# The output projection of a transformer layer, moved from a phase of its own into the attention loop

## The chip, the cores and the metric

The kernel runs on one core of a Trainium2 chip. The metric is the time of one execution on the device in microseconds. TensorE is called PE, VectorE DVE, ScalarE ACT, GpSimd POOL, and SyncE, which issues nearly all DMAs, SP.

## The reference

A layer on x (16 batches, 1024 tokens, width 256, float32): a modulated layer norm, attention with a residual, and a mixture of eight experts on the first two batches' tokens. Cut to what the change touches:

```
# q, k, v: [16 batches, 16 heads, 1024, 16], rotary embedding applied to q and k
scores = einsum('bhid,bhjd->bhij', q, k) / sqrt(16)
scores = scores * mask + (1 - mask) * -1e9            # causal
probs  = softmax(scores, axis=-1)
out    = einsum('bhij,bhjd->bhid', probs, v)          # then heads side by side: [16, 1024, 256]
out    = out @ Wo + bo
x      = x + ga * (h + out)                           # ga: a gate, one row of 256 per batch
```

## The kernel before, in words

`build` (L61) runs five phases, one after the other. Phase 0 prepares weights and the modulation rows, phase 1 makes q, k and v and stores them and the residual in DRAM, phase 2 (L717) is the attention, phase 3 (L1106) the output projection, phase 4 the experts. Each phase is a block in which the five engines run their own instruction lists, written out by hand in `@block.sync`, `@block.gpsimd` and so on, and meet by semaphores only. An engine works strictly in its list's order, so a wait holds up all that is queued behind it on that engine. At a phase's end all engines and outstanding DMAs meet.

Phase 2 works through 64 units: unit u = 4b + g is batch b and group g of four heads. Within a unit PE does two things in turn. For its own unit it computes transposed scores in ten pieces of up to 512 queries, four heads each (`scores_for_exp`, L1045). ACT takes the exponential of each (L992, from one of three PSUM banks), POOL zeroes the masked part of the six pieces on the diagonal, pieces 0, 1, 2, 7, 8 and 9 (`select`, L879), and two pieces later PE multiplies by the values (`weigh`, L1056). `weigh` of piece 7 therefore stands at the end of piece 9, the last of the unit, and those of pieces 8 and 9 in the next unit. The values carry columns of ones, so a head gives 16 rows of numerators and rows of the sum of its exponentials, the denominator. Between its score matmuls PE computes, for the unit two ahead, the plain scores whose row maxima DVE takes (`fill`, L1008, in 40 fillings, two for each of 20 slots; `largest`, L931). Slot 4 (`TURN`) holds no scores: its first filling transposes the maxima of the unit before (`turn_max`, L1039), its second is empty. The maxima are negated and split into three bf16 parts by DVE (L921) and POOL (`parts`, L888), and SP stores them to DRAM and loads them back as three more rows of q (`maxima`, L838), which is needed at the start of the next unit.

SP's list in a unit (`step`, L856) is: wait until the unit before has been weighed, load q, k and v for the unit four after it (nine DMAs for q and k, one for v, 2 MB), store the second half of the unit before, `maxima` of the next unit, store the first half of this unit (numerators and denominators unnormalised, in `att_d`, 512 KB a unit).

Phase 3 loads a batch of `att_d` (2 MB, double buffered) and the residual (1 MB), and goes through eight tiles of 128 tokens: PE transposes the tile's four groups (L1215), DVE takes the reciprocals of the denominators (L1180) and multiplies (L1184), PE transposes the product (two, L1223), ACT copies it (L1201), PE multiplies by the gated Wo, after a bf16 matmul for the bias (L1233, L1235), DVE adds the residual (L1190), and SP stores the batch.

Of the kernel before, what the change touches and what calls it, by code (L numbers as in the profile page):

```python
# [25 lines left out]
P = 128  # L26
# [34 lines left out]
def build(nc, a, out):  # L61
# [21 lines left out]
    max_d = nc.dram_tensor("neg_max", [NG, 3, HG * T, P], BF16, kind="Internal").ap()  # L83
    att_d = nc.dram_tensor("att", [B, NG, P, L], F32, kind="Internal").ap()
# [3 lines left out]
    with ExitStack() as outer:  # L88
# [12 lines left out]
        phase2(nc, B, L, ps, ident, mask, q_d, k_d, v_d, max_d, att_d)  # L101
        phase3(nc, B, L, D, ps, ident, wo, ones3, mods_d, out_bias_d, resid_d, att_d, sum_d, out)
# [614 lines left out]
def phase2(nc, B, L, ps, ident, mask, q_d, k_d, v_d, max_d, att_d):  # L717
    T = L // P
    DH = q_d.shape[3] // HG
# [44 lines left out]
    PS_A, PS_B, PS_O = 0, 4, 7  # L764
    BANKS = 3
# [3 lines left out]
    with ExitStack() as ctx:  # L769
# [13 lines left out]
        o_sb = sb("o_sb", [P, 2, HALF], F32)  # L783

# [9 lines left out]
        o_stored = many("p2_o_stored", 2)  # L794
        block = ctx.enter_context(nc.Block())

        LAST = B - 1

# [26 lines left out]
        def _(sp):  # L825
# [24 lines left out]

            def prologue():
                for n in range(UNITS):
                    load(unit(0, n))
                maxima(unit(0, 0))

            def step(un, ahead):  # L856
                b, g, u = un
                final = isinstance(b, int) and b == LAST
                if not (isinstance(b, int) and b == 0 and g == 0):
                    was = prior(un)  # L860
                    if not (final and g):

                        wait_apart(sp, pv_done, was[2] * NPC + NPC)
                        load(unit(was[0], was[1] + NG))
                    store(was, 1)
                if not (final and g == NG - 1):
                    maxima(unit(b, g + 1))
                store(un, 0)

            def epilogue():  # L870
                store(unit(LAST, NG - 1), 1)
                for c in range(2):
                    sp.wait_ge(o_stored[c], B * NG * DMA)
# [4 lines left out]
        def _(pool):  # L878
# [17 lines left out]

            def step(un, ahead):
                for i in range(NPC):
                    if diag(PIECES[i]):
                        select(un, i)  # L900
                    if i == 3 and ahead is not None:
                        parts(prior(ahead))
                if ahead is None and un[1] == NG - AHEAD:
# [7 lines left out]
            steps(pool, prologue, step)  # L911

        @block.vector
        def _(dve):
# [46 lines left out]
            def step(un, ahead):  # L961
                if ahead is not None:
                    whole(ahead)
                elif un[1] == NG - AHEAD:
# [6 lines left out]
            steps(dve, prologue, step)  # L971
# [35 lines left out]
        def _(pe):  # L1007
            def fill(un, n, first=False):  # L1008
# [30 lines left out]
            def turn_max(un):  # L1039
# [3 lines left out]
                             ident[:, :]).then_inc(turned, 1)  # L1043

# [38 lines left out]
            def step(un, ahead, first=False):  # L1083
                for i in range(NPC):
                    for h in range(HG):
# [17 lines left out]

def phase3(nc, B, L, D, ps, ident, wo, ones3, mods_d, out_bias_d, resid_d, att_d, sum_d, out):  # L1106
    T = L // P
    KC = D // P
    DH = D // HEADS
    SB = (sum_d.shape[0] - P) // L  # L1110
    PS_A, PS_T, PS_C = 0, 2, 4
    with ExitStack() as ctx:
        sb = lambda n, s, d: ctx.enter_context(nc.sbuf_tensor(n, s, d))
        sem = lambda n: ctx.enter_context(nc.semaphore(n))
        pair = lambda n: (sem(n + "0"), sem(n + "1"))
        att = sb("att_b", [P, 2, NG, L], F32)
        res = sb("res_b", [P, 2, T, D], F32)
        gate = sb("gate_b", [P, 2, D], F32)
        ob = sb("ob_b", [3, 2, D], BF16)
        wg = sb("wg", [P, 2, KC, D], F32)  # L1120
        rec = sb("rec", [P, 2, HEADS], F32)
        norm = sb("norm", [P, 2, D], F32)
        n_t = sb("n_t", [P, 2, KC, P], F32)
        x2 = sb("x2", [P, 2, T, D], F32)
        att_in, small_in, res_in = pair("p3_att_in"), pair("p3_small_in"), pair("p3_res_in")
        wg_done = sem("p3_wg")
        at_done, rec_done, norm_done = sem("p3_at"), sem("p3_rec"), sem("p3_norm")
        nt_done, nt_copied = sem("p3_nt"), sem("p3_nt_copied")
        c_done, x2_done = sem("p3_c"), sem("p3_x2")
        stored = pair("p3_stored")  # L1130
        block = ctx.enter_context(nc.Block())

        def loop(eng, work):
            for p in range(2):
                work(p, 0, p)
            for it in range(1, B // 2):
                for p in range(2):
                    work(it * 2 + p, it, p)

        def load(sp, b, p):  # L1140
            sp.dma_start(att[:, p], att_d[b].rearrange("g p t -> p g t")).then_inc(att_in[p], DMA)
            sp.dma_start(res[:, p], resid_d[b]).then_inc(res_in[p], DMA)
# [466 lines left out]
```

## Time and profile before

| | |
|---|---|
| time of 3 executions | 3256.54, 3257.68, 3258.6 us |
| the profiled execution | 3256.85 us, its span 3255.1 us |
| PE, DVE, ACT, POOL busy | 91%, 72%, 53%, 31% of the span |
| phase 2: first load of v to ACT's last copy | 767 to 2627 us |
| phase 3, to the first load of phase 4 | 2627 to 2915 us |

The profile is one execution. Busy shares are means over phases with different limits, so a stage is read by a table of stretches, and the order of things within a unit by the timeline. A number in square brackets after an instruction is the time that its engine stood idle before it, and what released it. The granted clock of PE is a share of 2.4 GHz; 0.50 is 1.2 GHz.

### The profile page before, as it was taken

Reading aid. Unit: us, or ns where it says so; the run is one execution under the profiler, and the core shown is the slowest. Engines: PE = TensorE matmul, PEld = TensorE weight load, DVE = VectorE, ACT = ScalarE, POOL = GpSimd, SP = SyncE. Lnnn points to the kernel's source line nnn. Section 1 sums busy time; section 2 is a strip of 40 time slices with the busy share of each in tenths; the row PEclk is TensorE's granted clock in tenths of the full one; section 3 lists DMA queues with packets and bytes.
Section 4 is the critical chain, followed back from the end, with each engine's and each line's share of the span. In section 5 each row is a group of like instructions: output and inputs, shape, how many; then the busy total and the mean of one; then the engine's idle time right before and its main releaser. Section 6 shows DMA issues by size and latency. Waiting matters only on the chain. (4 is left out here: it accounts for less than half of the span.)

```text
span 3255.1 us, 50330 instructions
## 1 busy us (share of the span) xinstructions
PE 2952.9 (91%) x18199; PEld 1403.3 (43%) x18199; DVE 2328.9 (72%) x3444; ACT 1713.4 (53%) x3591; POOL 1019.2 (31%) x1366
## 2 busy tenths in 40 slices
PE   2888998885999999999999999999999979975997
PEld 0444444441444444444444444444444347753664
DVE  5999999995777777777777777777777425543221
ACT  1444444430677777777777777777777731111111
POOL 3888888862122111112221111112221100003232
PEclk7999999996999999999999999999999989987999
DMA  2466666657244444444444444444444246663332
GB/s 77 138 180 191 191 191 191 184 156 175 55 95 93 95 100 100 100 96 92 94 95 92 97 100 100 100 96 90 95 92 92 48 173 259 259 230 110 78 100 56
DMA packets 175373, 403.11 MB, mean 124 GB/s; under 512 B 34556, under 2 KB 87202, under 8 KB 158518
## 3 DMA queue, kind: packets, MB, share of 16 engines
q1 hardware_dynamic: 168984, 391.37, 47.1%
q0 software_dynamic: 6144, 8.52, 1.5%
q8 instruction: 147, 2.41, 0.3%
q14 instruction: 98, 0.80, 0.1%
HBM read 240.65 MB, written 161.31 MB: 123 GB/s over the span
## 5 line engine op out<-in xcount | busy, mean ns | idle before, releaser
L946 DVE TENSOR_REDUCE mx<-ps 128x2 f32<-128x1024 f32 (+3 forms) x1216 | 1371.2, 1166 | 396.6 <-PE ps L1034 301.3
L992 ACT ACTIVATE prob<-ps 128x512 f32<-128x512 f32 (+1 forms) x2560 | 1251.4, 561 | 539.0 <-PE ps L1052 530.0
L1027 PE MATMUL ps<-k_rows,q_rows 96*128 96x512 bf16 (+3 forms) x3072 | 909.9, 332 | 40.6 <-DMA k_rows<-k_parts 33.1
L1052 PE MATMUL ps<-q_rows,k_rows 99*128 99x512 bf16 (+3 forms) x3072 | 908.5, 329 | 14.5 <-ACT prob L992 6.0
L885 POOL TENSOR_SCALAR_AFFINE_SELECT prob<-prob 128x512 f32<-128x512 f32 x512 | 318.6, 634 | 1453.8 <-ACT prob L992 1453.8
L1071 PE MATMUL ps<-prob,v_rows 128*32 128x512 f32 (+3 forms) x6144 | 628.6, 497 | 0.0
L1052 PEld LDWEIGHTS ps<-q_rows,k_rows 99*128 99x128 bf16 x3072 | 273.3, 98 | 598.8 <-ACT prob L992 359.8
L688 PE MATMUL ps<-w_all,x_t 128*128 128x512 f32 (+1 forms) x1024 | 427.9, 543 | 0.0
L1027 PEld LDWEIGHTS ps<-k_rows,q_rows 96*128 96x128 bf16 x3072 | 290.4, 98 | 269.8 <-DVE mx L946 60.4
L1034 PE MATMUL ps<-mask_b,unit_b 128*128 128x128 bf16 (+2 forms) x1408 | 348.5, 248 | 0.0
L1071 PEld LDWEIGHTS ps<-prob,v_rows 128*32 128x32 f32 x6144 | 134.7, 108 | 245.7 <-ACT prob L992 122.8
L688 PEld LDWEIGHTS ps<-w_all,x_t 128*128 128x128 f32 x1024 | 183.5, 200 | 125.4 <-issue 104.0
L481 DVE TENSOR_TENSOR qr<-m 128x256 f32<-128x256 f32 x256 | 224.2, 958 | 4.4
L641 POOL TENSOR_TENSOR stage<-rest,stage 128x512 bf16<-128x512 f32 x128 | 167.5, 1308 | 119.3 <-ACT stage L575 119.2
L1201 ACT COPY n_t<-ps 128x256 f32<-128x256 f32 x128 | 47.6, 372 | 232.7 <-PE ps L1223 232.7
L1469 DVE SCALAR_TENSOR_TENSOR y<-ps,gx,gate 128x256 f32<-128x256 f32 x32 | 15.5, 484 | 195.7 <-PE ps L1560 192.3
L1034 PEld LDWEIGHTS ps<-mask_b,unit_b 128*128 128x128 bf16 x1408 | 139.2, 99 | 22.8
L1235 PE MATMUL ps<-wg,n_t 128*128 128x256 f32 x512 | 145.7, 407 | 0.0
L561 ACT COPY v_st<-ps 128x256 f32<-128x256 f32 x128 | 47.7, 373 | 178.1 <-PE ps L688 178.1
L675 PE MATMUL ps<-ident,xn 128*128 128x128 f32 x256 | 55.9, 304 | 87.1 <-DVE xn L461 87.1
L1190 DVE TENSOR_TENSOR x<-ps,res_b 128x256 f32<-128x256 f32 x128 | 54.3, 425 | 106.2 <-PE ps L1235 106.2
L1560 PE MATMUL ps<-w,hid 128*128 128x256 f32 x512 | 119.1, 386 | 0.0
(143 smaller groups left out, 2707.4 us busy)
## 6 DMA issues: line engine op xcount, KB each, us to landing
k_rows<-k_parts SPq DMA_DIRECT2D x384, 128.0 KB, 7.5
v_ones<-v_st SPq DMA_DIRECT2D x64, 512.0 KB, 9.0
v_rows<-v_ones SPq DMA_DIRECT2D x64, 512.0 KB, 9.5
att<-o_sb SPq DMA_DIRECT2D x128, 256.0 KB, 3.2
att_b<-att SPq DMA_DIRECT2D x16, 2048.0 KB, 10.9
q_parts<-stage SPq DMA_DIRECT2D x192, 128.0 KB, 2.4
k_parts<-stage SPq DMA_DIRECT2D x192, 128.0 KB, 2.4
q_rows<-q_parts SPq DMA_DIRECT2D x64, 384.0 KB, 4.6
```

The source lines that it names most:

```text
L481: ins = dve.tensor_tensor(dst[:, :, :, :, e], src(m1)[:, :, :, :, e], src(m2)[:, :, :, :, 1 - e], ALU.add)
L641: pool.tensor_tensor(stage[:, p, 2, :, t * P:(t + 1) * P], rest[:, t % 2, :].rearrange("p (a n) -> p a n", a=4), stage[:, p, 1, :, t * P:( ...
L688: ins = pe.matmul(o, x_t[:, t % 2, k, :], w_all[:, k, lo:hi], start=False, stop=(k == KC - 1))
L885: pool.affine_select(out=own, in_=own, compare_op=ALU.is_ge, fill=0.0, base=0, pattern=[[0, HG], [1, P]], channel_multiplier=-1).then_inc( ...
L946: dve.tensor_reduce(dst, src, AX.X, ALU.max).then_inc(a_free, 1)
L992: nc.scalar.activation(prob[:, (g * NPC + i) % RING, h, 0:w], src, ACT.Exp).then_inc(exp_done, 1)
L1027: ins = pe.matmul(ps[:, at, col:col + w], q[0:ROWS, g, h, i * P:(i + 1) * P], k[0:ROWS, g, h, k0:k0 + w], start=(r == 0), stop=True, skip_ ...
L1034: ins = pe.matmul(own, unit_b[:, :], mask_b[:, :].rearrange("p (o n) -> p o n", o=1) .to_broadcast([P, per, P]), start=False, stop=True, s ...
L1052: ins = pe.matmul(ps[:, PS_B + bank(g, n), at:at + w], k[0:AUG, g, h, j * P:(j + 1) * P], q[0:AUG, g, h, q0:q0 + w], start=True, stop=True)
L1071: ins = pe.matmul(ps[32 * h:32 * h + 32, PS_O, col:col + w], v[:, g, j, h, :], prob[:, (g * NPC + i) % RING, h, at:at + w], start=(j == 0) ...
L1235: ins = pe.matmul(o, n_t[:, r % 2, k, :], wg[:, p, k, :], start=False, stop=(k == KC - 1))
L1560: ins = pe.matmul(o, hid[:, f, c * P:(c + 1) * P], w2[:, e % 2, f, :], start=False, stop=(f == FT - 1))
```

## The change

Phase 3 is gone; its work is done inside phase 2. The numerators and denominators are not loaded as tokens by heads and transposed, but fetched out of `att_d` in the layout that the projection's stationary operand wants: 8 heads x 16 numerator rows make the 128 partitions of `num`, twice. The denominators of a batch come as one tile of 128 x 128 (`den`), DVE inverts it (`invert`), SP stores it to DRAM and loads it back with each head's row spread over that head's 16 partitions (`rec_b`), and POOL multiplies (`normalise`). The matmul then takes `num` as it is. The unit of the projection is a job j: two tiles of 128 tokens, four jobs to a batch, into one PSUM bank.

Where it all stands: SP fetches batch b - 1 in unit (b, 0), after `maxima`; saves and spreads the reciprocals in unit (b, 1), before and after `maxima`; stores the finished rows of batch b - 2 in unit (b, 2), after its last store. DVE inverts at slot 5 and makes the gated Wo at slot 12 of unit (b, 1), and adds a job's rows at slot 4. POOL normalises batch b - 1 in unit (b, 1) between `parts` and the selection of piece 7. PE does job u - 6 in unit u, in the empty second filling of slot 4, and slot 6, which uses that bank next, waits for the addition. The last six jobs and all that batch 15 needs follow the loop.

The diff, without declarations and without the removed phase 3:

```diff
         LAST = B - 1
+        BEHIND = 6
+        PAIRS = T // 2
+        JOBS = B * PAIRS
+        assert PAIRS == NG and TURN % 2 == 0
+        def job_of(u):
+            return u - BEHIND if u >= BEHIND else None
...
+            def fetch(b):
+                p, half = b % 2, b // 2
+                for c in range(2):
+                    sp.wait_ge(o_stored[c], (b + 1) * NG * DMA)
+                rows = att_d[b].rearrange("g (h n) t -> (g h) n t", h=HG)
+                reuse(sp, rec_done, b)
+                sp.dma_start(den[:, :], rows[:, DH, :].rearrange("h (x t) -> h x t", t=P)).then_inc(den_in, DMA)
+                reuse(sp, out_done, (b - 1) * PAIRS)
+                for k in range(KC):
+                    sp.dma_start(num[:, p, k, :], rows[8 * k:8 * k + 8, 0:DH, :]).then_inc(num_in[p], DMA)
+                sp.dma_start(gate[:, p], mods_d[b, M_GA, :].partition_broadcast(P)).then_inc(small_in[p], DMA)
+                sp.dma_start(ob[:, p], out_bias_d[b]).then_inc(small_in[p], DMA)
+                reuse(sp, x2_stored[p], half * DMA)
+                sp.dma_start(res[:, p], resid_d[b]).then_inc(res_in[p], DMA)
+            def save_reciprocals(b):
+                sp.wait_ge(rec_done, b + 1)
+                sp.dma_start(rec_d[b % 2].rearrange("h (x t) -> (h x) t", t=P), rec[:, :]).then_inc(rec_saved, DMA)
+            def spread_reciprocals(b):
+                sp.wait_ge(rec_saved, b * DMA + DMA)
+                reuse(sp, att_ready, b * PAIRS)
+                for k in range(KC):
+                    src = rec_d[b % 2, 8 * k:8 * k + 8, :].rearrange("h (o t) -> h o t", o=1).to_broadcast([8, DH, L])
+                    sp.dma_start(rec_b[:, k, :], src).then_inc(rec_in, DMA)
+            def store_rows(b):
+                sp.wait_ge(x2_done, (b + 1) * PAIRS)
+                dst = sum_d[b * L:(b + 1) * L] if b < SB else out[b]
+                sp.dma_start(dst.rearrange("(t p) d -> p t d", p=P), res[:, b % 2]).then_inc(x2_stored[b % 2], DMA)
...
+                if g == 1 and b >= 1:
+                    save_reciprocals(b - 1)
                 if not (final and g == NG - 1):
                     maxima(unit(b, g + 1))
+                if g == 0 and b >= 1:
+                    fetch(b - 1)
+                if g == 1 and b >= 1:
+                    spread_reciprocals(b - 1)
                 store(un, 0)
+                if g == 2 and b >= 2:
+                    store_rows(b - 2)
             def epilogue():
                 store(unit(LAST, NG - 1), 1)
-                for c in range(2):
-                    sp.wait_ge(o_stored[c], B * NG * DMA)
+                fetch(LAST)
+                save_reciprocals(LAST)
+                spread_reciprocals(LAST)
+                store_rows(LAST - 1)
+                store_rows(LAST)
+                for p in range(2):
+                    sp.wait_ge(x2_stored[p], DMA * (B // 2))
...
+            def normalise(b):
+                pool.wait_ge(num_in[b % 2], (b // 2 + 1) * KC * DMA)
+                pool.wait_ge(rec_in, (b + 1) * KC * DMA)
+                for r in range(PAIRS):
+                    at = slice(r * 2 * P, (r + 1) * 2 * P)
+                    pool.tensor_tensor(num[:, b % 2, :, at], num[:, b % 2, :, at], rec_b[:, :, at], ALU.mult) \
+                        .then_inc(att_ready, 1)
             def step(un, ahead):
                 for i in range(NPC):
                     if diag(PIECES[i]):
                         select(un, i)
                     if i == 3 and ahead is not None:
                         parts(prior(ahead))
+                    if i == 6 and un[1] == 1 and un[0] >= 1:
+                        normalise(un[0] - 1)
                 if ahead is None and un[1] == NG - AHEAD:
                     parts(unit(LAST, NG - 1))
...
-            def whole(un, first=False):
+            def invert(b):
+                dve.wait_ge(den_in, b * DMA + DMA)
+                reuse(dve, rec_saved, b * DMA)
+                dve.reciprocal(rec[:, :], den[:, :]).then_inc(rec_done, 1)
+            def gated(b):
+                dve.wait_ge(small_in[b % 2], (b // 2 + 1) * (2 * DMA))
+                reuse(dve, out_done, (b - 1) * PAIRS)
+                for k in range(KC):
+                    ins = dve.tensor_tensor(wg[:, b % 2, k, :], wo[:, k, :], gate[:, b % 2, :], ALU.mult)
+                ins.then_inc(wg_done, 1)
+            def add_rows(j, bank):
+                b, r = j // PAIRS, j % PAIRS
+                rows = res[:, b % 2, 2 * r:2 * r + 2, :]
+                dve.wait_ge(res_in[b % 2], (b // 2 + 1) * DMA)
+                dve.wait_ge(out_done, j + 1)
+                dve.tensor_tensor(rows, ps[:, bank, :].rearrange("p (r n) -> p r n", r=2), rows, ALU.add) \
+                   .then_inc(x2_done, 1)
+            def whole(un, now=None, first=False):
                 for s in range(NS):
-                    if s == 2 and not first:
+                    if now is not None and now[1] == 1 and now[0] >= 1 and s == 5:
+                        invert(now[0] - 1)
+                    if now is not None and now[1] == 1 and now[0] >= 1 and s == 12:
+                        gated(now[0] - 1)
+                    if un is not None and s == 2 and not first:
                         finish(prior(un))
-                    if s != TURN:
+                    if un is not None and s != TURN:
                         largest(un, s)
-                    elif not first:
+                    elif un is not None and not first:
                         negate(prior(un))
+                    if s == TURN and now is not None and job_of(now[2]) is not None:
+                        add_rows(job_of(now[2]), PS_OUT)
...
+                whole(ahead, now=un)
+            def epilogue():
+                for j in range(JOBS - BEHIND, JOBS):
+                    if j == LAST * PAIRS:
+                        invert(LAST)
+                        gated(LAST)
+                    add_rows(j, PS_TAIL[j % 2])
...
+                j = job_of(u - AHEAD)
                 if s == TURN:
                     if not first and half == 0:
                         pe.wait_ge(a_free, u * NR + s - 1)
                         turn_max(prior(un))
+                    if half == 1 and j is not None:
+                        project(j, PS_OUT)
                     return
                 if half == 0 and s - 2 == TURN:
                     reuse(pe, m_left, u)
+                    if j is not None:
+                        pe.wait_ge(x2_done, j + 1)
                 elif half == 0:
                     reuse(pe, a_free, u * NR + (real(s - 2) + 1 if s >= 2 else s - 1))
...
+            def project(j, bank):
+                b, r = j // PAIRS, j % PAIRS
+                if r == 0:
+                    pe.wait_ge(wg_done, b + 1)
+                    pe.wait_ge(small_in[b % 2], (b // 2 + 1) * (2 * DMA))
+                pe.wait_ge(att_ready, j + 1)
+                for t in (2 * r, 2 * r + 1):
+                    o = ps[:, bank, (t % 2) * D:(t % 2) * D + D]
+                    pe.matmul(o, ones3[:, :], ob[:, b % 2, :], start=(t % 2 == 0), stop=False, skip_group_check=True)
+                    for k in range(KC):
+                        ins = pe.matmul(o, num[:, b % 2, k, t * P:(t + 1) * P], wg[:, b % 2, k, :], start=False,
+                                        stop=(k == KC - 1), skip_group_check=True)
+                ins.then_inc(out_done, 1)
...
+                        if ahead is None and n == 9:
+                            pe.wait_ge(x2_done, job_of(un[2]))
+                            project(job_of(un[2]), PS_OUT)
...
                 weigh(unit(LAST, NG - 1), i)
+            for j in range(JOBS - BEHIND, JOBS):
+                pe.wait_ge(x2_done, j - 1)
+                project(j, PS_TAIL[j % 2])
```

## Rows read from the trace of the kernel before

**Rows 1.** The page: busy tenths of PE and its granted clock in 40 slices.
```profile
PE   2888998885999999999999999999999979975997
PEclk7999999996999999999999999999999989987999
```

**Rows 2.** By stretches: us, busy PE, PEld, DVE, ACT, POOL, clock, DMA, GB/s.
```profile
2431.09:2459.29 28.20, 28.14 (x220) 11.60 (x216) 21.99 (x23) 20.53 (x42) 5.62 (x10) 1.00 0.48 96
2629.00:2914.60 285.60, 253.66 (x1408) 191.52 (x1408) 149.53 (x416) 47.62 (x128) 0.00 (x0) 0.96 0.65 243
```

**Rows 3.** Timeline of PE in the projection phase: start us, us, engine, line.
```profile
2650.95 0.28 PE L1233 MATMUL ps<-ob_b,ones 3*128 3x256 bf16 x1
...
2652.12 0.60 PE L1215 MATMUL ps<-ident,att_b 128*128 128x128 f32 x4
...
2652.88 0.28 PE L1233 MATMUL ps<-ob_b,ones 3*128 3x256 bf16 x1
```

**Rows 4.** Timeline at the projection phase's two ends.
```profile
2626.41 0.58 ACT L980 COPY o_sb<-ps 128x512 f32<-128x512 f32 x1 [1.87 <-PE ps L1071]
...
2909.93 0.39 SPq L1150 DMA_DIRECT2D out<-x  x1
2914.63 0.37 SPq L1312 DMA_DIRECT2D x_all<-sum_rows  x1
```

**Rows 5.** Chain that ended last, just after the projection phase: start us, us.
```profile
2914.63 8.33 DMA x_all<-sum_rows
```

**Rows 6.** The same chain in the last phase.
```profile
2985.13 0.21 PE ps L1558
2985.34 3.65 PE ps L1560 x16
```

**Rows 7.** Timeline of PE within one unit, and at its end.
```profile
2437.84 0.22 PE L1034 MATMUL ps<-mask_b,unit_b 128*128 128x128 bf16 x1
2438.13 0.28 PE L1052 MATMUL ps<-q_rows,k_rows 99*128 99x256 bf16 x1
...
2458.29 1.06 PE L1071 MATMUL ps<-prob,v_rows 128*32 128x512 f32 x8
```

**Rows 8.** Groups of instructions by line: busy us, mean ns of one, idle before.
```profile
L641 POOL TENSOR_TENSOR stage<-rest,stage 128x512 bf16<-128x512 f32 x128 | 167.5, 1308 | 119.3 <-ACT stage L575 119.2
...
L474 DVE TENSOR_TENSOR m<-ps,rope 128x512 f32<-128x512 f32 x128 | 86.8, 678 | 7.6 <-PE ps L688 7.6
...
L234 DVE RECIPROCAL e<-e 16x256 f32<-16x256 f32 x1 | 1.7, 1741 | 0.0
```

**Rows 9.** Timeline of SP and POOL within the same unit.
```profile
2437.24 1.23 SPq L835 DMA_DIRECT2D q_rows<-q_parts  x3
...
2442.24 0.43 SPq L841 DMA_DIRECT2D neg_max<-m  x1
2451.83 0.25 SPq L843 DMA_DIRECT2D q_rows<-neg_max  x1
...
2453.32 0.63 POOL L885 TENSOR_SCALAR_AFFINE_SELECT prob<-prob 128x512 f32<-128x512 f32 x1 [12.92 <-ACT prob L992]
```

**Rows 10.** DMA issues by tile: size, median us to landing.
```profile
v_rows<-v_ones SPq DMA_DIRECT2D x64, 512.0 KB, 9.5
...
res_b<-resid SPq DMA_DIRECT2D x16, 1024.0 KB, 12.8
```

**Rows 11.** The tile xin, one load of 1024 KB: its landings.
```profile
DMA to landing us min/median/max: 5.4/7.7/8.9
```

**Rows 12.** Timeline at the one long pause of PE in the attention phase.
```profile
2600.12 1.91 PE L1052 MATMUL ps<-q_rows,k_rows 99*128 99x512 bf16 x4 [4.62 <-DMA q_rows<-neg_max]
```

**Rows 13.** Table by stretches about that pause (columns as in rows 2).
```profile
2596.00:2597.00 1.00, 0.00 (x0) 0.00 (x0) 0.00 (x0) 0.00 (x0) 0.42 (x1) 1.00 0.00 0
2597.00:2598.00 1.00, 0.00 (x0) 0.00 (x0) 0.00 (x0) 0.00 (x0) 0.00 (x0) 0.84 0.11 25
...
2604.00:2605.00 1.00, 0.96 (x6) 0.41 (x4) 0.00 (x0) 0.53 (x2) 0.00 (x0) 0.75 0.00 0
```

More of the change, by code:

```diff
@@ L83, in build @@
     max_d = nc.dram_tensor("neg_max", [NG, 3, HG * T, P], BF16, kind="Internal").ap()
+    rec_d = nc.dram_tensor("rec_den", [2, HEADS, L], F32, kind="Internal").ap()
     att_d = nc.dram_tensor("att", [B, NG, P, L], F32, kind="Internal").ap()
@@ L100, in build @@
         phase1(nc, x, ps, ident, rope, w_all, bias3, ones3, mods_d, resid_d, q_d, k_d, v_d)
-        phase2(nc, B, L, ps, ident, mask, q_d, k_d, v_d, max_d, att_d)
-        phase3(nc, B, L, D, ps, ident, wo, ones3, mods_d, out_bias_d, resid_d, att_d, sum_d, out)
+        phase2(nc, B, L, D, ps, ident, mask, wo, ones3, mods_d, out_bias_d, resid_d, q_d, k_d, v_d, max_d, att_d, rec_d,
+               sum_d, out)
         phase4(nc, a, SB, ps, ident, mask, ones3, mods_d, b2_d, tok_d, sum_d, out)
@@ L713, in _, with phase2 @@
             run(pe, lambda fr: None, both, lambda bk: turn_qk(bk, T - 1))
-def phase2(nc, B, L, ps, ident, mask, q_d, k_d, v_d, max_d, att_d):
+def phase2(nc, B, L, D, ps, ident, mask, wo, ones3, mods_d, out_bias_d, resid_d, q_d, k_d, v_d, max_d, att_d, rec_d,
+           sum_d, out):
     T = L // P
+    KC = D // P
+    SB = (sum_d.shape[0] - P) // L
     DH = q_d.shape[3] // HG
@@ L764, in phase2 @@
     PS_A, PS_B, PS_O = 0, 4, 7
+    PS_OUT = PS_A + 1
+    PS_TAIL = (PS_A + 3, PS_A + 1)
     BANKS = 3
@@ L783, in phase2 @@
         o_sb = sb("o_sb", [P, 2, HALF], F32)
+        num = sb("num", [P, 2, KC, L], F32)
+        rec_b = sb("rec_b", [P, KC, L], F32)
+        den = sb("den", [P, P], F32)
+        rec = sb("rec", [P, P], F32)
+        res = sb("res_b", [P, 2, T, D], F32)
+        gate = sb("gate_b", [P, 2, D], F32)
+        ob = sb("ob_b", [3, 2, D], BF16)
+        wg = sb("wg", [P, 2, KC, D], F32)
         qk_in, v_in, m_in = many("p2_qk_in", UNITS), many("p2_v_in", UNITS), many("p2_m_in", UNITS)
@@ L794, in phase2 @@
         o_stored = many("p2_o_stored", 2)
+        num_in, den_in, res_in, small_in = many("p2_num_in", 2), sem("p2_den_in"), many("p2_res_in", 2), many("p2_small_in", 2)
+        rec_done, rec_saved, rec_in = sem("p2_rec"), sem("p2_rec_saved"), sem("p2_rec_in")
+        att_ready, wg_done = sem("p2_att_ready"), sem("p2_wg")
+        out_done, x2_done, x2_stored = sem("p2_out"), sem("p2_x2"), many("p2_x2_stored", 2)
         block = ctx.enter_context(nc.Block())
         LAST = B - 1
+        BEHIND = 6
[4 more added lines that the diff above has]
+            return u - BEHIND if u >= BEHIND else None
         def unit(b, n):
@@ L909, in prologue @@
                 parts(unit(0, 0))
-            steps(pool, prologue, step)
+            steps(pool, prologue, step, lambda: normalise(LAST))
         @block.vector
@@ L961, in step @@
             def step(un, ahead):
-                if ahead is not None:
-                    whole(ahead)
-                elif un[1] == NG - AHEAD:
+                if ahead is None and un[1] == NG - AHEAD:
                     final = unit(LAST, NG - 1)
@@ L967, in step @@
                     negate(final)
+                whole(ahead, now=un)
[5 more added lines that the diff above has]
+                    add_rows(j, PS_TAIL[j % 2])
             dve.tensor_copy(unit_b[:, :], ident[:, :]).then_inc(consts, 1)
             dve.tensor_copy(mask_b[:, :], mask[:, 384:512]).then_inc(consts, 1)
-            steps(dve, prologue, step)
+            steps(dve, prologue, step, epilogue)
         @block.scalar
```

123 lines of the change are left out of this document (removed).

## The prediction

> **What bounds the kernel now.** I read the page from the top and then went into the stages. TensorE (PE) is the busiest engine, and from the eleventh to the thirty-second of the 40 slices it is at 9 tenths throughout, and so is its granted clock [rows 1]: that is the attention phase. The table by stretches sets one unit of that phase (one batch, one group of four heads, 2431.09 to 2459.29) beside the whole projection phase (from 2629) [rows 2]. The reader is to see that a unit lasts 28.20 us, that PE is busy for 28.14 of it, and that DVE has 6.2, ACT 7.7 and POOL 22.6 us of slack. So an operation added to DVE, ACT or POOL in a unit is free unless somebody waits for it, and one added to PE is paid. The projection phase that is removed is 285.6 us by that row. In its steady part a tile of 128 tokens takes 1.93 us (2650.95 to 2652.88 [rows 3]).
>
> **What goes.** In the trace of before, ACT's last copy of the attention ends at 2626.99, and the phase after the projection starts its first load at 2914.63 [rows 4]. Between lie 287.6 us, all on the path.
>
> **What comes at the end instead (the tail).** From 2626.99 on, step by step: the last store of half a unit 2.4 us (an estimate: half of the 4.7 below, for a quarter of the bytes); six fetches are issued, at 0.4 us and more each, while the numerators (1 MB) and the residual (1 MB) fill the queue, and the reciprocals' save lands behind them, 8.6 us after the first issue (x_all, 2 MB, took 8.33 [rows 5]); the spread DMAs 7.2 (below); POOL's first multiplication 1.3; four jobs on PE; the last addition 0.7; the store of the last rows and the change of phase 4.7 (2909.93 to 2914.63 [rows 4]). A job is 2.24 us (next part), and PE restarts from a pause of over 10 us at half clock (as after the pause of [rows 12, 13]), so I count the first double, half a microsecond extra on the second: 4 x 2.24 + 2.4 = 11.4. The sum is 2.4 + 8.6 + 7.2 + 1.3 + 11.4 + 0.7 + 4.7 = 36.3, with 0.9 for waits 37.2. The removed phase is therefore worth 287.6 - 37.2 = 250.4 us.
>
> **What the loop gets on PE.** 58 of the 64 jobs run inside the loop, one per unit from the seventh unit on, at the second (empty) filling of the TURN slot; six are in the tail. A job is two tiles of one bf16 matmul and four f32 instructions. In the last phase the same kinds stand 0.21 us and 3.65/16 = 0.228 us apart [rows 6], so a tile is 0.21 + 4 x 0.228 = 1.12 and a job 2.24 us; by the projection phase's own rows a tile takes 1.17 (2650.95 to 2652.12 [rows 3]), so 2.34. The transpositions (six per tile) are really gone. In front of the place where the job goes, PE is not quite full: between 2437.84 and 2438.13 a matmul of 0.06 us is followed by a wait, 0.23 us, and about 0.1 us is lost before it [rows 7], because the banks of the scores for the exponential are waited for. The job fills about 0.3 us of that. I take 2.24 - 0.3 = 1.95 us; the ends are 1.6 (all small waits of the unit swallowed) and 2.34. 58 x 1.95 = 113 us (93 to 136).
>
> **DVE, ACT, and the banks.** DVE gets one addition 128x512 per unit (0.68 us, as its multiplication out of PSUM of that shape), and per batch a reciprocal of 128 elements (half of 256 elements' 1.74 us, so 0.9 to 1.0) and two products of 256 elements, under 0.7 each [rows 8]. With 6.2 us of slack all are covered; only the two products, put before a reduction for which PE has a slack of about half a microsecond, can hold PE up: 0.1 us per batch, 1 us in all. Slot 6 waits for the addition in its bank: the addition ends near 9.4 us after the unit's start, slot 6 is written near 11.0. ACT loses its copies n_t and gains nothing.
>
> **SP and the DMAs.** In a unit (times from its start at 2431.09 [rows 9]) SP waits until 6.15, issues ten loads and a store, then the save of the maxima at 11.15, then stands until that has landed behind 2 MB of loads at 20.74, reloads, and stores the first half right after. In groups of kind g = 0 the fetches follow at 21: six issues, 3 to 5 us, 2.2 MB, through by about 34, while the next loads are at 36. What is queued behind them is the store of the first half, whose buffer is needed 14 us into the next unit. In g = 2 the store of finished rows, 1 MB, lies in the same gap. Both cost nothing; without the gap they would cost their issue time.
>
> **The wait that takes the place.** In each unit with g = 1 POOL multiplies the numerators (`normalise`), and it is queued on POOL ahead of the selection of piece 7, and PE is queued behind that selection. The chain: PE's job ends at 8.6, DVE's addition at 9.4, its reciprocal at 10.4, so the save goes out at 11.2 without delay. It and the save of the maxima land at 20.9 (64 KB more than before), because they stand behind the loads. The two spread DMAs, 512 KB each into 128 partitions, go out from 21.3. The trace shows no such transfer; nearest are 4.7 for a lone store of 1 MB [rows 4], 8.3 for a load of 2 MB [rows 5], 7.7 (median) for a load of 1 MB in some traffic, 9.5 for the 512 KB load inside the loop, 12.8 for 1 MB behind 2 MB [rows 10, 11]. The queue is empty but it is a load: I take 7.2, just under its nearest row, so 28.5. POOL's two-input operation of 512 elements lasts 1.31 us [rows 8]; four, with their waits, 5.3: 33.8. The selection of piece 7 takes 0.63 [rows 9]: 34.5. PE wants it at 2458.29, that is at 27.20 [rows 7], plus the job's 1.95: 29.15. PE stands still for 5.4 us. It can't be hidden by what comes later, since PE was full.
> The clock: in the one place where PE paused like this within the phase, 4.62 us before 2600.12, the granted clock fell from 1.00 to 0.50 (2.4 to 1.2 GHz) during the pause and came back at 2604.5 [rows 12, 13]. 4.4 us of work at half speed cost 2.2 us. So 7.6 us per batch, and `normalise` runs 15 times inside the loop: 114 us. Ends: 2.9 x 15 = 44 (landing 4.7, clock kept) and 13.2 x 15 = 198 (landing 12.8).
>
> The Trainium skill, "DMA: Bandwidth & Descriptors", section "Rules for kernel authors", says that a transfer uses no more engines than the outermost dimension of its access patterns has steps, so one with fewer than 16 leaves engines unused. The source of each spread DMA (and of each numerator DMA) begins with 8 heads, which by that rule leaves it half of the 16 engines. No row of before shows such a transfer; the third rival prices it.
>
> **Sum**, against the profiled execution's own 3256.85 us (span 3255.1 and 1.75 around it; the median of the runs is 0.8 above): 3256.85 - 250.4 + 113 + 1 + 114 = 3234.5, say 3235.
>
> **Rivals.**
> First, the short pause: the spread DMAs land like the lone store, 4.7 us, PE stands 2.9 us, and the clock, which in [rows 13] was still at 1.00 for the first two of the pause's microseconds, does not fall. Then 15 x 2.9 = 44 and the tail is 2.5 shorter: 3256.85 - 252.9 + 113 + 1 + 44 = 3162. For it: the queue is empty. Against it: loads of 1 MB never landed under 5.4 us [rows 11].
> Second, on the other side, the slow spread: every microsecond by which the two DMAs land later is paid 15 times. The change turns slower when the batch's loss passes (250.4 - 113 - 1)/15 = 9.1 us, which is a landing of 8.7 us. With the 9.5 us of the load inside the loop [rows 10] PE stands 7.7, loses 9.9 per batch, 149 in all, the tail is 2.3 longer: 3256.85 - 248.1 + 113 + 1 + 149 = 3272. For it: each row is read sixteen times out of DRAM, which no row prices. Against it: that 9.5 is spent mostly behind other loads.
> Third, half of the engines: 1 MB at half the pace is 2 MB at the whole, 8.3 us [rows 5]. The pause is 6.5, the loss 8.7, 15 x 8.7 = 131, the tail 1.1 longer: 3256.85 - 249.3 + 113 + 1 + 131 = 3253, no change. This is the result that the skill's rule gives.
> Fourth, that the projection costs nothing in the loop, as a filling between waits: 3235 - 113 = 3122. PE's 28.14 of 28.20 us speak against it; 2%.
>
> **Chances.** Forecast 52%, own range 3205 to 3265 (landing 6.0 to 8.2 us, job 1.7 to 2.3); short pause 15%; slow spread 15%; half of the engines 13%; the fourth and anything else 5%. What a measurement here can tell from no change is 0.2%, 6.5 us: below 3251 is faster, above 3264 slower. Faster: four fifths of the forecast, the short pause, the fourth, half of the third, 0.68; the same: 0.14; slower: most of the slow spread and the edge of the others, 0.18. The range runs from the short pause to past the slow spread, 3161 to 3285.
>
> **What would show it.** A unit of kind 0, 2 or 3 lasts 30.15 us (1.6 to 2.3 over 28.20). One of kind 1 lasts about 37.7, with one PE gap of 5.4 us before line `weigh`'s matmuls, released by POOL's selection, right behind four POOL multiplications of 1.3 us which begin 28 to 29 us into the unit, released by the spread DMAs; the clock is at 0.50 for some 4 us after it. The end of the attention to the first load of the last phase: 37 us. The forecast is wrong if the multiplications end before 28 us, if PE never waits for a selection, if the units without a gap are above 31 us, or if SP issues the fetches so late that the maxima's reload is what PE waits for.

## The result, and the profile after

The changed kernel takes 3295.62 us (median of four executions, 3294.47 to 3300.33), the kernel before 3258.14 beside it (3256.54 to 3259.22): ratio 1.0118, 95% interval 1.0101 to 1.0136, so 37 us slower. The forecast was 3235, and the time lies outside its range of 3161 to 3285. The profiled execution took 3300.33 us, its span is 3298.6 us, and PE's mean granted clock 0.930 (0.952 before).

The first look is the page of the kernel after, its slices as in [rows 1].

```profile
PE   2888889885998998999998999999989999945997
PEclk7999999995998999999999999999999999977999
```

From the eleventh slice to the thirty-fifth PE's line shows four eights among the nines, and the clock's line one, where before both stood at nine throughout the middle of the attention. So PE no longer runs through. The table by stretches (us, then PE, PEld, DVE, ACT and POOL busy, clock, DMA share, GB/s, as in [rows 2]) sets a unit of kind 2 beside 30 us that hold a pause:

```profile
2366.47:2396.88 30.41, 30.41 (x227) 13.27 (x226) 22.69 (x24) 20.76 (x43) 5.65 (x11) 1.00 0.45 89
2306.00:2336.00 30.00, 22.59 (x165) 9.29 (x166) 17.26 (x19) 15.25 (x31) 7.91 (x9) 0.89 0.28 76
```

The first is a unit of 30.41 us in which PE is busy throughout; it was 28.20 [rows 2]. The second misses 7.4 us of PE. The waits by engine, line and releaser (us, times, the longest one) give the sum over the program:

```profile
PE ps L1208 <- POOL prob L957: 117.5, 14, 12.6
POOL num L975 <- DMA rec_b<-rec_den: 334.2, 16, 30.6
```

L1208 is `weigh`, L957 `select`, L975 `normalise`. The timeline of one batch shows the chain (start us, us, engine, line, what, idle time before it). First SP:

```profile
2302.19 0.43 SPq L895 DMA_DIRECT2D rec_den<-rec  x1
2302.66 0.43 SPq L867 DMA_DIRECT2D neg_max<-m  x1
2310.74 0.26 SPq L869 DMA_DIRECT2D q_rows<-neg_max  x1
2311.09 1.22 SPq L903 DMA_DIRECT2D rec_b<-rec_den  x2
```

then POOL and PE:

```profile
2321.60 4.92 POOL L975 TENSOR_TENSOR num<-num,rec_b 128x512 f32<-128x512 f32 x4 [20.03 <-DMA rec_b<-rec_den]
2326.48 2.40 POOL L957 TENSOR_SCALAR_AFFINE_SELECT prob<-prob 128x512 f32<-128x512 f32 x4
```

```profile
2319.63 0.22 PE L1156 MATMUL ps<-mask_b,unit_b 128*128 128x128 bf16 x1
2327.26 1.93 PE L1208 MATMUL ps<-prob,v_rows 128*32 128x512 f32 x8 [7.41 <-POOL prob L957]
...
2332.44 1.07 PE L1208 MATMUL ps<-prob,v_rows 128*32 128x384 f32 x16
```

SP's save of the reciprocals goes out without delay, the spread DMAs 8.9 us after it, and POOL, which needs them, starts 10.51 us later (2311.09 to 2321.60); in the mean of the 14 units with a pause it starts 10.9 us later (10.5 to 12.1). Its four multiplications end at 2326.52, the first of four overdue selections some 0.6 us later, and PE has stood for 7.41 us. The same `weigh` of eight matmuls that took 1.06 us [rows 7] then takes 1.93. The table by stretches (columns as above) through this place:

```profile
2314.00:2315.00 1.00, 1.00 (x11) 0.20 (x9) 1.00 (x2) 0.67 (x2) 0.00 (x0) 1.00 0.53 131
2317.00:2318.00 1.00, 1.00 (x10) 0.16 (x8) 1.00 (x2) 0.75 (x2) 0.00 (x0) 1.00 0.50 119
2323.00:2324.00 1.00, 0.00 (x0) 0.00 (x0) 0.00 (x0) 0.00 (x0) 1.00 (x1) 0.98 0.00 0
2324.00:2325.00 1.00, 0.00 (x0) 0.00 (x0) 0.00 (x0) 0.00 (x0) 1.00 (x2) 0.50 0.00 0
```

Two things are to be seen: the clock falls from 2.4 to 1.2 GHz during the pause, and while the spread DMAs alone are under way the queue uses half of the 16 engines' time (0.50 to 0.53) and moves 119 to 131 GB/s.

At the end of the attention, what answers to [rows 4] (one timeline, ACT and SP, then POOL and PE):

```profile
2907.44 0.59 ACT L1097 COPY o_sb<-ps 128x512 f32<-128x512 f32 x1 [1.87 <-PE ps L1208]
...
2914.15 0.32 SPq L895 DMA_DIRECT2D rec_den<-rec  x1
2926.15 1.23 SPq L903 DMA_DIRECT2D rec_b<-rec_den  x2
...
2936.99 4.93 POOL L975 TENSOR_TENSOR num<-num,rec_b 128x512 f32<-128x512 f32 x4 [30.65 <-DMA rec_b<-rec_den]
2938.40 0.37 PE L1176 MATMUL ps<-ob_b,ones 3*128 3x256 bf16 x1 [25.93 <-POOL num L975]
...
2957.16 0.37 SPq L1319 DMA_DIRECT2D x_all<-sum_rows  x1
```

From 2908.03, the copy's end, to 2957.16 are 49.1 us, where 287.6 stood before.

The account of the two profiled executions: 3256.85 - 287.6 + 49.1 = 3018.35. The attention phase starts 2.6 us later and ends 281.0 us later (2908.03 against 2626.99), so it has grown by 278.4. The pauses lengthen 14 units by 151.7 us in all, 10.83 in the mean. The first, whose spread DMAs go out 2 us later than most and which has no job ahead of the pause, is 15.6 longer than a unit of 28.20; the other 13 are 9.3 to 11.9 longer than one of 30.41. Of the 10.83, 117.5/14 = 8.4 are the wait, and some 2.4 are left for the stretch at half clock. So 278.4 - 151.7 = 126.7 us are left for the 58 jobs, 2.18 each. With 0.9 for a longer last phase: 3018.35 + 2.6 + 278.4 + 0.9 = 3300.25, against 3300.33.

### The profile page after: what moved, and what is told of

Its sections match the earlier page's. It is cut to its first block and busy times, and to the rows that moved or that the text cites. A ratio compares the mean times of both kernels' runs of the same rounds, so it can differ in the third digit from the quotient of the medians.

```text
span 3298.6 us, 48163 instructions
## 1 busy us (share of the span) xinstructions
PE 2885.9 (87%) x17431; PEld 1330.0 (40%) x17431; DVE 2246.3 (68%) x3140; ACT 1679.3 (51%) x3463; POOL 1097.7 (33%) x1430
## 5 line engine op out<-in xcount | busy, mean ns | idle before, releaser
L1109 ACT ACTIVATE prob<-ps 128x512 f32<-128x512 f32 (+1 forms) x2560 | 1264.5, 559 | 804.2 <-PE ps L1189 796.4
L1189 PE MATMUL ps<-q_rows,k_rows 99*128 99x512 bf16 (+3 forms) x3072 | 925.8, 332 | 9.8 <-ACT prob L1109 4.8
L957 POOL TENSOR_SCALAR_AFFINE_SELECT prob<-prob 128x512 f32<-128x512 f32 x512 | 318.6, 637 | 1355.7 <-ACT prob L1109 1355.7
L1208 PE MATMUL ps<-prob,v_rows 128*32 128x512 f32 (+3 forms) x6144 | 640.6, 505 | 117.7 <-POOL prob L957 117.5
L1208 PEld LDWEIGHTS ps<-prob,v_rows 128*32 128x32 f32 x6144 | 135.4, 109 | 364.4 <-issue 246.6
L975 POOL TENSOR_TENSOR num<-num,rec_b 128x512 f32<-128x512 f32 x64 | 78.8, 1263 | 334.2 <-DMA rec_b<-rec_den 334.2
L1050 DVE TENSOR_TENSOR res_b<-ps,res_b 128x512 f32<-128x512 f32 x64 | 44.3, 692 | 201.7 <-PE ps L1178 201.7
L1178 PE MATMUL ps<-wg,num 128*128 128x256 f32 x512 | 147.5, 411 | 0.0
```

The costliest lines, as they stand in the source:

```text
L957: pool.affine_select(out=own, in_=own, compare_op=ALU.is_ge, fill=0.0, base=0, pattern=[[0, HG], [1, P]], channel_multiplier=-1).then_inc( ...
L1109: nc.scalar.activation(prob[:, (g * NPC + i) % RING, h, 0:w], src, ACT.Exp).then_inc(exp_done, 1)
L1178: ins = pe.matmul(o, num[:, b % 2, k, t * P:(t + 1) * P], wg[:, b % 2, k, :], start=False, stop=(k == KC - 1), skip_group_check=True)
L1189: ins = pe.matmul(ps[:, PS_B + bank(g, n), at:at + w], k[0:AUG, g, h, j * P:(j + 1) * P], q[0:AUG, g, h, q0:q0 + w], start=True, stop=True)
L1208: ins = pe.matmul(ps[32 * h:32 * h + 32, PS_O, col:col + w], v[:, g, j, h, :], prob[:, (g * NPC + i) % RING, h, at:at + w], start=(j == 0) ...
```

## The experiments

The theory after the result: the loss is the pause of PE in each unit with g = 1, caused by POOL's order (normalisation ahead of the selection of piece 7) and sized by the spread DMAs' landing, which is long because their pattern has only 8 outer steps. The rivals: the loss is contention or the work itself and would stay without the wait; or the landing is long because each row is read sixteen times. The kernel before took 3257.16 us beside late, spread16, rows8 and rows16, and 3257.51 beside the others.

**late: the same work, but the wait ahead of nobody.** POOL normalises after the selection of piece 9.

```diff
-                    if i == 6 and un[1] == 1 and un[0] >= 1:
-                        normalise(un[0] - 1)
+                if un[1] == 1 and un[0] >= 1:
+                    normalise(un[0] - 1)
```

> Only the place of POOL's four multiplications changes: they stand behind the selection of piece 9, at the end of the unit, instead of ahead of that of piece 7. Theory A (the change is slower because a selection queues behind them): the long units shrink from 39.78 to 30.4 us, 15 x 9.37 = 141 us go, 3295 - 141 = 3155 us, and no gap of PE over 1 us is left in the loop. Rival B (the wait only moves): the first job of the batch waits for the multiplications in the next unit, or the selection of piece 0 does, the gap shows there, and the time stays above 3230 us. Rival C (the 9.4 us are contention of the larger DMA traffic with the other engines): units stay long without a gap released by POOL, 3270 or more.

Measured: 3147.32 us (3144.83 to 3148.22), ratio to before 0.9662 (0.9645 to 0.9678). The timeline of POOL in a unit with g = 1, whose spread DMAs were issued at 2201.12:

```profile
2209.53 0.63 POOL L957 TENSOR_SCALAR_AFFINE_SELECT prob<-prob 128x512 f32<-128x512 f32 x1 [1.03 <-ACT prob L1109]
2212.05 4.96 POOL L975 TENSOR_TENSOR num<-num,rec_b 128x512 f32<-128x512 f32 x4 [1.89 <-DMA rec_b<-rec_den]
2216.96 1.81 POOL L957 TENSOR_SCALAR_AFFINE_SELECT prob<-prob 128x512 f32<-128x512 f32 x3
```

The stretch that holds it (columns as before):

```profile
2186.00:2216.00 30.00, 29.93 (x223) 12.95 (x222) 23.66 (x27) 20.30 (x42) 8.63 (x13) 1.00 0.60 127
```

The spread lands as late as ever, 10.9 us after its issue, POOL still waits for it, and three selections are late behind it, but PE is busy for 29.93 of 30 us at full clock: what is queued behind POOL now is needed only later. From one unit's start to the next, the units with g = 1 last 30.41 us here, like the others. The two lines' place costs 3295.6 - 3147.3 = 148 us, against 151.7 summed from the units of the trace. That is shown: the pauses are the whole of the loss, and in the loop the same DMAs and multiplications without them cost nothing.

**spread16, rows8, rows16: why the landing is long.** spread16 puts the 16 rows of a head outermost in the two numerator and the two spread DMAs; partition (row, head) instead of (head, row), and Wo's rows are loaded in the same order, so the matmul sums the same products.

```diff
-            (wo[:, :, :], a["L0_attn_Wo"].rearrange("(k p) n -> p k n", p=P)),
+            (wo[:, 0, :], a["L0_attn_Wo"][0:P].rearrange("(h m) n -> m h n", h=8)),
+            (wo[:, 1, :], a["L0_attn_Wo"][P:2 * P].rearrange("(h m) n -> m h n", h=8)),
...
+                    sp.dma_start(num[:, p, k, :], rows[8 * k:8 * k + 8, 0:DH, :].rearrange("h n t -> n h t")) \
...
-                    src = rec_d[b % 2, 8 * k:8 * k + 8, :].rearrange("h (o t) -> h o t", o=1).to_broadcast([8, DH, L])
+                    src = rec_d[b % 2, 8 * k:8 * k + 8, :].rearrange("(o h) t -> o h t", o=1).to_broadcast([DH, 8, L])
```

> The 16 rows of a head are the outer dimension of the sources of the numerators' and the spread's DMAs instead of the 8 heads; partitions are in the order (row, head), and Wo is loaded in the same order. Same bytes, same descriptors of 4 KB, reciprocals' rows still read 16 times each. Theory A (eight outer steps use half of the DMA engines): the DMA share during the spread is near 1.0 instead of 0.50, its landing falls from 10.5 to 6 or 7 us, PE's gap by 4 us, with a shorter stretch at half clock: 15 x 4 to 5 us and 8 us in the tail, 3295 - 75 = 3220 us (3205 to 3240). Rival B (it is slow because each row is read sixteen times): the landing stays at 10 us, 3290 us or more.

Measured: 3236.97 us (3233.75 to 3238.07), ratio 0.9934 (0.9918 to 0.9951). The timeline of SP and POOL, and of PE, in one batch:

```profile
2272.07 1.17 SPq L905 DMA_DIRECT2D rec_b<-rec_den  x2
...
2278.99 4.93 POOL L977 TENSOR_TENSOR num<-num,rec_b 128x512 f32<-128x512 f32 x4 [16.41 <-DMA rec_b<-rec_den]
...
2284.65 1.93 PE L1210 MATMUL ps<-prob,v_rows 128*32 128x512 f32 x8 [3.80 <-POOL prob L959]
```

and its DMA engines meanwhile, by stretches:

```profile
2275.00:2276.00 1.00, 1.00 (x11) 0.20 (x9) 1.00 (x2) 0.68 (x2) 0.00 (x0) 1.00 0.88 213
2277.00:2278.00 1.00, 1.00 (x12) 0.65 (x9) 0.65 (x1) 1.00 (x3) 0.00 (x0) 1.00 0.93 268
```

With the same bytes the share goes from 0.50 to about 0.9, the rate doubles, and the landing falls from 10.5 to 6.9 us, close to the 7.2 of the prediction. A paused unit is 7.07 us too long in the mean (14 of them, 99 us), the wait alone 4.7: the clock falls here too, and takes its 2.4.

The Trainium skill, "DMA: Bandwidth & Descriptors", section "Rules for kernel authors", states that the slowest dimension of the patterns sets how many engines a DMA can use, and advises putting one whose size is a multiple of 16 outermost. The two traces agree: 0.50 of the engines with 8 outer steps, 0.88 to 0.93 with 16.

rows8 and rows16 load `att_d` in place of the reciprocals, so no row is read twice: 8 heads by 16 rows in the one, 128 plain rows in the other. Both leave the normalisation by the denominators out.

```diff
-                    sp.dma_start(rec_b[:, k, :], src).then_inc(rec_in, DMA)
+                    heads = att_d[b].rearrange("g (h n) t -> (g h) n t", h=HG)                    # rows8
+                    sp.dma_start(rec_b[:, k, :], heads[8 * k:8 * k + 8, 0:DH, :]).then_inc(rec_in, DMA)
...
+                    sp.dma_start(rec_b[:, k, :], att_d[b, k, :, :]).then_inc(rec_in, DMA)         # rows16
```

> The spread's DMAs load numerator rows (8 heads by 16 different rows) instead of the reciprocals' rows repeated; the normalisation is thereby left out of the result. Eight outer steps as before, no repeated reads. Theory A (engines): landing as with the repeated rows, 10 us at a DMA share of 0.50, time 3290 to 3300. Rival B (repeated reads): landing 7 us or less, time about 3240.

> The spread's DMAs load 128 plain rows each, with no repeated reads and 128 outer steps; the normalisation is left out of the result. Theory A (engines): landing 5 to 6 us at a share near 1.0, time 3215 to 3235. Rival B (repeated reads): the same as rows8, both fast. If rows8 is in the middle, both count. Here PE's gap should be about 4 us, which also shows whether a pause of that length lets the clock fall.

Measured: rows8 3282.4 us, rows16 3211.72 (one execution each). The timelines of the two loads and of POOL behind them, in rows8:

```profile
2301.25 1.22 SPq L903 DMA_DIRECT2D rec_b<-att  x2
...
2310.95 4.92 POOL L975 TENSOR_TENSOR num<-num,rec_b 128x512 f32<-128x512 f32 x4 [19.30 <-DMA rec_b<-att]
```

and in rows16, with PE:

```profile
2248.06 0.81 SPq L902 DMA_DIRECT2D rec_b<-att  x2
...
2253.47 4.94 POOL L974 TENSOR_TENSOR num<-num,rec_b 128x512 f32<-128x512 f32 x4 [14.82 <-DMA rec_b<-att]
...
2259.15 1.13 PE L1207 MATMUL ps<-prob,v_rows 128*32 128x512 f32 x8 [2.22 <-POOL prob L956]
```

The landings make a square. Each is the time from the issue of the spread DMAs to POOL's start, the mean of the 14 units with a pause:

| landing (PE's mean wait in 14 pauses), us | 8 outer steps | 16 or more |
|---|---|---|
| each row read 16 times | 10.9 (8.4), after | 6.8 (4.7), spread16 |
| each row read once | 9.6 (7.4), rows8 | 5.4 (3.1), rows16 |

The outer steps are worth 4.1 to 4.2 us of landing, the repeated reading 1.2 to 1.4, and PE's mean waits say the same (3.7 to 4.3, 1.0 to 1.6). So both rivals of the prediction were at work, the half engines with some three quarters of the effect. rows8 and rows16 stand on one execution each, but on 14 landings, which lie at 9.2 to 10.3 and 5.2 to 6.0 us.

**late_spread16 and tail: both edits, and the end.** The first is late with spread16's edit. The second also issues the last batch's residual behind its spread DMAs.

```diff
-                reuse(sp, x2_stored[p], half * DMA)
-                sp.dma_start(res[:, p], resid_d[b]).then_inc(res_in[p], DMA)
+                if b != LAST:
+                    fetch_residual(b)
...
+                fetch_residual(LAST)        # in the epilogue, after spread_reciprocals(LAST)
```

> Both edits together. Without the pauses in the loop (theory A) the faster spread can be worth something only in the tail, where the landing of the numerators, the saved reciprocals and the spread stands on the path: 3.6 us for the spread and 2 to 4 for the save behind the numerators: 3147 - 6 = 3141 us (3138 to 3145). If the two edits' gains added up (148 and 59 us from 3295.6) it would be 3089: that would speak against their being the same wait.

> As late_spread16, and in the tail the last residual is fetched behind the spread instead of ahead of the reciprocals' save. If the save lands late because it queues behind 1 MB of residual (theory A) it lands 3 us earlier, and the addition, which needs the residual, is later still: 3 us less, 3138 us. Rival: the residual is then what the last additions wait for, no gain.

Measured: late_spread16 3139.44 us (3138.56 to 3139.79), ratio 0.9636 (0.9623 to 0.965); tail 3137.41 (3135.67 to 3139.74), ratio 0.9631 (0.9618 to 0.9644), the fastest version, 120 us under the kernel before. The two can't be told apart by their times. Once nobody waits for the spread in the loop, its pattern is worth only what it saves at the end. The timeline of SP in tail's end, where the attention's last copy ends at 2755.16:

```profile
2761.27 0.32 SPq L901 DMA_DIRECT2D rec_den<-rec  x1
2765.54 1.17 SPq L909 DMA_DIRECT2D rec_b<-rec_den  x2
...
2793.22 0.37 SPq L1326 DMA_DIRECT2D x_all<-sum_rows  x1
```

The end takes 38.1 us instead of 49.1 (48.1 in late, 40.3 in late_spread16). The save of 64 KB lands in 4.3 us instead of 12.0, and that is the work of both edits: it still takes 10.6 in late, whose patterns are those of the changed kernel, 7.2 in late_spread16 with the other patterns of the numerators and the spread, and 4.3 once the residual is issued behind it. That last step makes the end 2.2 us shorter in the two traces, too little for the times to tell.

**warm: what the clock takes of a pause.** The changed kernel with 30 useless matmuls of 512 columns on PE ahead of the `weigh` that waits, in the 15 units with g = 1.

```diff
+            def keep_busy(un, ahead, count):
+                pe.wait_ge(a_free, ahead[2] * NR + real(18) + 1)
+                for _ in range(count):
+                    pe.matmul(ps[:, PS_A, :], q[0:ROWS, un[1], 0, 0:P], k[0:ROWS, un[1], 0, 0:512], start=True,
+                              stop=True, skip_group_check=True)
...
+                        if ahead is not None and un[1] == 1 and un[0] >= 1 and n == NEXP - 1:
+                            keep_busy(un, ahead, 30)
```

> The changed kernel with 30 useless matmuls of 512 columns (6.5 us, results never read) on PE just ahead of the piece that waits for the selection, in the 15 units of kind g = 1. They keep PE busy during its pause and shorten nothing that it waits for. If the clock's fall costs what the traces suggest (10.8 us of lengthening against 8.4 us of pause, 2.4 us each), the clock stays at 1.00, the long units are 2.4 us shorter, and the time is 3295.6 - 14 x 2.4 = 3262 us, although PE does more. Rival: the 2.4 us are not the clock's but later waits; then the time stays at 3295 or rises.

Measured: 3280.01 us (3271.95 to 3282.55), ratio 1.006 (1.0045 to 1.0075), 16 us under the changed kernel, about half of what was expected. The timeline of PE in one batch where it worked, and in one where it didn't:

```profile
2302.13 6.65 PE L1186 MATMUL ps<-k_rows,q_rows 96*128 96x512 bf16 x30 [0.54 <-DVE mx L1029]
2309.09 1.07 PE L1215 MATMUL ps<-prob,v_rows 128*32 128x512 f32 x8 [0.32 <-POOL prob L957]
```

```profile
993.01 6.65 PE L1186 MATMUL ps<-k_rows,q_rows 96*128 96x512 bf16 x30 [0.54 <-DVE mx L1029]
1003.91 1.94 PE L1215 MATMUL ps<-prob,v_rows 128*32 128x512 f32 x8 [4.25 <-POOL prob L957]
```

In the first the clock holds: the same `weigh` takes 1.07 us instead of 1.93. In the second the spread landed in 11.6 us and four microseconds of pause were left, enough for the half clock. Eleven paused units are 7.8 to 8.9 us too long, 8.3 in the mean, where the same eleven are 10.3 too long in the changed kernel, so some 2 us of a pause are the clock's; the other three stayed above 11, with 2.4 to 4.3 us of pause left behind the useless matmuls. The mean of the 14 is 9.28, so the pauses give back 14 x 1.55 = 22 us. The fifteenth unit with g = 1, in the last batch, had no pause to fill, and there the useless matmuls are paid:

```profile
2825.68 6.65 PE L1186 MATMUL ps<-k_rows,q_rows 96*128 96x512 bf16 x30 [0.54 <-DVE mx L1029]
2832.26 1.06 PE L1215 MATMUL ps<-prob,v_rows 128*32 128x512 f32 x8
```

That unit is 7.0 us longer than in the changed kernel, so 15 us are left of the 22, near the measured 16. The expectation had left this unit out. That useless matmuls make the kernel faster is the sign that the clock takes its part of each pause.

**half_job: is the job paid in full?** late, with the four float32 matmuls of each job's second tile left out.

```diff
...
-                    for k in range(KC):
+                    for k in range(KC if t % 2 == 0 else 0):
...
```

> From the kernel late, with the four f32 instructions of each job's second tile left out (its rows then hold bias and residual only). If a job costs its matmuls' time on a full PE (4 x 0.228 = 0.91 us), a unit is 30.41 - 0.91 = 29.5 us and the time 3147 - 64 x 0.91 = 3089 us. Rival: half a job hides in the small waits of the unit, 28.6 us and 3040.

Measured: 3089.54 us (one execution), 57.8 under late, for 64 jobs 0.90 us each; four float32 instructions of 0.228 us are 0.91 [rows 6]. So the matmuls of half a job are paid in full, and the rival, by which they hide in the small waits of the unit, is out.

## Why the prediction was wrong

The mechanism was right, and the sizes of three of its terms were not. By the prediction's own steps:

- **What goes**: 287.6 us, as said.
- **SP, DVE, ACT, the banks**: right. The save goes out 12 us into the unit (11.2 said), the spread DMAs at 21.0 (21.3 said), counted from the unit's start as in [rows 9], where SP's loads begin at 6.15. `late` shows with 29.93 of 30 us, and with units of 30.41 us of every kind, that none of the added operations, fetches and stores holds PE up.
- **The wait that takes the place**: right in place, order and releaser, too small in size. **This is the step that failed: "it is a load: I take 7.2, just under its nearest row".** The landing is 10.5 in the batch shown and 10.9 in the mean of 14. Everything else in that chain came near what was said: POOL's four multiplications take 4.92 (5.3), PE wants piece 7 at 29.7 (29.15), the clock costs 2.4 (2.2). A pause costs 10.83 instead of 7.6, and there are 14 and not 15: unit 61, the last batch's, issues no loads, so its save lands at once (the spread goes out 2.6 us after it), and PE never waits there. In all 151.7 against 114: +37.7. The 3.7 us of landing are more than the whole difference per pause (3.2). I took a number just under a 1-MB load's median, and left the pattern's 8 outer steps to a rival of 13% and the sixteenfold reading to one of 15%. The square above shows that both apply, and that they add up; a rival priced with both causes (8.3 by [rows 5], and about 1 for the second, for which the rows of before had no price) lands near the second rival's 3272, on the right side of no change. The range failed with it: the prediction gave the pauses the ends 44 and 198 us, and the measured 151.7 lies between them, but 198 with its other terms is 3318, and the range stopped at 3285. spread16, the DMA that I had in mind, lands in 6.9 and measures 3237. That this is so close to the forecast is partly luck: its pauses take 99 us (114 said) and its end 41.1 (37.2), while a job costs more than it said here too.
- **What the loop gets on PE**: 2.18 us per job against 1.95, 126.7 against 113: +13.7, still inside its bounds. The timeline of PE in the kernel after shows a job, from L1176 to the next score matmul:

```profile
2366.74 0.28 PE L1176 MATMUL ps<-ob_b,ones 3*128 3x256 bf16 x1
2366.94 1.13 PE L1178 MATMUL ps<-wg,num 128*128 128x256 f32 x4
2368.01 0.28 PE L1176 MATMUL ps<-ob_b,ones 3*128 3x256 bf16 x1
2368.22 1.13 PE L1178 MATMUL ps<-wg,num 128*128 128x256 f32 x4
2369.18 0.27 PE L1189 MATMUL ps<-q_rows,k_rows 99*128 99x256 bf16 x1
```

  It occupies 2.44 us, 0.2 more than 2.24, and about that much of the small wait beside it went.
- **The tail**: 49.1 against 37.2, +11.9: the save of the reciprocals takes 12.0 us behind 2 MB of numerators and residual, not 8.6 from the first issue (it was issued 4 us after it), and the spread 10.8 instead of 7.2. These two are +11.0; the four jobs take 13.4 instead of 11.4, since PE stays at half clock into the second, and the small terms are 1.1 less.
- The products' 1 us is inside the jobs' remainder: -1. A later start of the attention and a longer last phase, which nothing in the change explains: +3.5.

Together: 3234.5 + 37.7 + 13.7 + 11.9 - 1 + 3.5 = 3300.3, the profiled execution. The rival on the other side had its point at "a landing of 8.7 us", and the landing lay beyond it. Its arithmetic held; its chance was too low, because I asked only what each rival would cost alone.

The projection inside the loop is a gain by itself: without the pauses 3147, and 3137 with a shorter end. How much of that comes from the missing transpositions and how much from the place isn't settled; the new layout in a phase of its own wasn't tried.

## What to carry to other kernels

A wait that depends on a DMA belongs on its engine behind all that another engine needs soon; here two lines' place was worth 148 us, and no change to the DMA itself came near that (59 in spread16; 84 in rows16, which leaves out the normalisation). Before a new DMA is given a landing time, its pattern is compared with that of the row it is priced by: outer steps and repeated source rows too, and where two causes each lengthen it, the case with both gets a chance of its own. A pause of a busy PE is priced with its clock: here about 2 us on top of each but the shortest.

## What the runs showed that was not expected

- A DMA of 8 x 16 rows of 4 KB out of DRAM moves about 125 GB/s at a share of 0.50 of the engines, and one of 16 x 8 rows twice that. Rows of one address read sixteen times cost 1.2 to 1.4 us on 1 MB.
- The clock fell even after a pause of 2.22 us, and only when PE was already back at work. In rows16, by stretches:

```profile
2259.00:2260.00 1.00, 0.85 (x8) 0.19 (x8) 0.00 (x0) 0.00 (x0) 1.00 (x3) 1.00 0.00 0
2260.00:2261.00 1.00, 1.00 (x9) 0.52 (x6) 0.00 (x0) 0.15 (x1) 0.76 (x2) 0.51 0.00 0
2263.00:2264.00 1.00, 1.00 (x7) 0.60 (x6) 1.00 (x1) 0.59 (x1) 0.00 (x0) 0.79 0.00 0
```

  The pause ends at 2259.15, and the clock is at 0.51 from 2260 on until it comes back in 2263. So a pause cut from 8.4 to 3.1 us in the mean still took 1.8 on top of itself (a paused unit of rows16 is 4.86 us too long).
- One pause of the same trace was a little shorter, 2.01 us, and there the clock held:

```profile
1124.76 1.07 PE L1207 MATMUL ps<-prob,v_rows 128*32 128x512 f32 x8 [2.01 <-POOL prob L956]
1126.00:1127.00 1.00, 1.00 (x12) 0.73 (x11) 0.00 (x0) 0.76 (x2) 0.37 (x1) 1.00 0.00 0
```

  The unit is 2.07 us too long, the pause and nothing on top. The thirteen others of rows16, from 2.22 us up, cost 1.6 us or more on top of the wait.
